# A delta-rule attention and mixture-of-experts layer, redesigned: attention state kept over x, paired inverses in small tiles, accumulating transfers, experts by batch, norms at the end

## The chip, the cores and the metric

One core of one Trainium2 chip. The time is that of one execution on the device in microseconds (us); of the kernel before, the median of three runs counts. Its engines are TensorE (PE: matmuls; PEld are its weight loads), VectorE (DVE), ScalarE (ACT), GpSimd (POOL) and SyncE (SP, which only issues transfers here).

## What is computed

```python
# B=2 sequences, S=2048 tokens, D=128; H=4 heads, DK=128, DV=32
q, k, v, beta = x @ Wq, x @ Wk, x @ Wv, sigmoid(x @ Wb)
k = k * rsqrt(sum(k*k, -1) + 1e-12);  q = q * DK**-0.5
# per head, over the tokens t of a sequence:
delta = (v_t - k_t^T S) * beta_t;  S = S + k_t delta^T;  o_t = q_t^T S
o = o * rsqrt(mean(o*o, -1) + 1e-5) * norm_w;  o = o * (g * sigmoid(g))   # g = x @ Wg
x1 = layernorm(x + o @ Wo)
# experts: E=8, F=448, top 2 of 8, capacity 640 for each batch and expert
probs = softmax(x1 @ gate_w.T);  slots = tokens of an expert in their order, first 640
y = (silu(slots @ w1) * (slots @ w3)) @ w2
out = layernorm(x1 + sum of y * probs over the token's two experts)
```

## The kernel before

The program is one block with a hand-written instruction stream for each engine, joined by semaphores.

**Attention (`phase_a`, 16 steps).** A step handles one chunk of 128 tokens of both sequences, so 8 pairs of sequence and head (`U = 8`). Within a chunk the recurrence is solved as a triangular system: A holds k times k below the diagonal, its inverse TT is built from 16x16 blocks on POOL (`solve`, 15 rounds of two operations, after a trip of the diagonal blocks through HBM), then joined on PE to 32, 64 and 128 wide (`z_32`, `w_32`, `z_64`, `w_64`, `z_128`, `w_128`, with a copy on DVE or ACT after each). The state St is kept as keys times deltas, 128x32 for each of the eight, and four groups of eight matmuls run over it and K (`ks`, `qs`, `t_r`, `k_d`, with `p_d` for the outputs inside the chunk). `step` writes PE's order by hand: what fills PSUM for chunk p+1 (`kt`, `k_tok`, `vb`, `kk`, `gate_t`, `qt`, `kq`) alternates with the inverse of chunk p and with the output of chunk p-1. An iteration of PE's loop holds two steps. All of this is float32, which the trace shows as two PE records for each matmul.

**Routing.** The output part of a step projects with Wo, adds x, normalises, turns x1 over (`x1_t`), forms the logits, takes the top two (`route`), counts tokens by expert with a triangular matmul (`cum`), and computes slots and gates (`place`). POOL scatters each token's row (four indirect transfers a step, `scatter`) into the table `slots_in`.

**Experts (16 units: eight experts for batch 0, then eight for batch 1).** A unit loads 640 slots and the expert's weights, turns the rows over (`flip`), forms both hidden matrices in 4 pieces of 112 features and 2 halves of 320 slots, each with three float32r matmuls (high and low halves of the split numbers: 48 matmuls of 320 columns), ACT takes Silu, DVE multiplies, and `down` multiplies with w2 (20 float32 matmuls, 40 records). PE has two PSUM banks for each of the two matrices. POOL writes the rows of the result back to the table `results` (five indirect transfers a unit, `send_back`).

**End.** `combine` reads x1 and the two expert rows of each token, adds them with the gates, and normalises; the combine of batch 0 runs beside the experts of batch 1, that of batch 1 after them, with a power on POOL (`c_rstd`) in each of 8 groups.

## Time and profile before

| what | us |
|---|---|
| median of 3 runs | 921.78 |
| range of the runs | 912.18 to 927.48 |
| span of the profiled execution | 911.5 |
| busy in it: PE / DVE / ACT / POOL | 752.7 / 419.9 / 337.6 / 398.9 |

The rows further down come from that one profiled execution. A row of the windows view gives for a stretch its length, each engine's busy time with its number of instructions, the clock that TensorE was granted as a share of 2.4 GHz, the share of the transfer engines and GB/s. A row of the timeline gives start, duration, engine, line, operation, output and inputs, shape, number of instructions merged, and in brackets the idle time before with what ended it. A row of the chain gives start, duration and what the chain that ended last was in.

### The profile page before, as it was taken

Reading aid. Unit: us, or ns where it says so; the run is one execution under the profiler, and the core shown is the slowest. Engines: PE = TensorE matmul, PEld = TensorE weight load, DVE = VectorE, ACT = ScalarE, POOL = GpSimd, SP = SyncE. Lnnn points to the kernel's source line nnn. Section 1 sums busy time; section 2 is a strip of 40 time slices with the busy share of each in tenths; the row PEclk is TensorE's granted clock in tenths of the full one; section 3 lists DMA queues with packets and bytes.
Section 4 is the critical chain, followed back from the end, with each engine's and each line's share of the span. In section 5 each row is a group of like instructions: output and inputs, shape, how many; then the busy total and the mean of one; then the engine's idle time right before and its main releaser. Section 6 shows DMA issues by size and latency. Waiting matters only on the chain.

```text
span 911.5 us, 19015 instructions
## 1 busy us (share of the span) xinstructions
PE 752.7 (83%) x6000; PEld 653.8 (72%) x6000; DVE 419.9 (46%) x1604; ACT 337.6 (37%) x1042; POOL 398.9 (44%) x794
## 2 busy tenths in 40 slices
PE   5398988988988989989989889753999999999700
PEld 4387877877877878778778778743888888887600
DVE  3135365455455453464462653413444546566444
ACT  3235345335335334254252451212343433434200
POOL 4444565474474562654653645121242433435321
PEclk9769799779779777788785795556999999999955
DMA  7342102111111111202201111012132324524042
GB/s 281 86 136 38 36 17 50 36 35 29 35 32 31 35 34 21 43 14 40 43 14 35 23 31 35 7 54 86 60 119 79 99 89 140 156 92 144 30 121 81
DMA packets 122469, 58.46 MB, mean 64 GB/s; under 512 B 73153, under 2 KB 115521, under 8 KB 122433
## 3 DMA queue, kind: packets, MB, share of 16 engines
q1 hardware_dynamic: 117824, 48.54, 20.7%
q0 software_dynamic: 4608, 9.48, 3.1%
q8 instruction: 18, 0.29, 0.1%
q14 instruction: 19, 0.15, 0.1%
HBM read 30.65 MB, written 27.34 MB: 64 GB/s over the span
## 4 chain that ended last, share of the span: by engine, by line
PE 55%; DVE 18%; issue 11%; ACT 8%; POOL 3%; DMA 3%; SPq 1%; DVEq 1%; ACTq 0%; POOLq 0%
PE ps L772 8%; PE ps L782 8%; PE ps L626 6%; PE ps L513 5%; PE ps L643 4%; PE ps L651 4%; DVE A L1167 3%; DVE hb L1243 3%; PE ps L523 3%; PE ps L615 3%; ACT hs L973 3%; PE ps L561 3%; PE ps L588 2%; ACT junk L827 2%; PE ps L635 2%
## 5 line engine op out<-in xcount | busy, mean ns | idle before, releaser
L1462 POOL DMA_INDIRECT results<-ye,row x80 | 81.4, 1018 | 160.3 <-ACT ye L979 124.9
L1243 DVE TENSOR_TENSOR hb<-ps,hs 112x320 f32<-112x320 f32 x128 | 62.8, 491 | 95.4 <-ACT hs L973 92.1
L772 PE MATMUL ps<-xeTh,w13h 128*112 128x320 f32 x256 | 88.1, 344 | 9.9 <-DVE hb L1243 7.4
L1397 POOL TENSOR_TENSOR prod<-ab,xs 64x15 f32<-64x15 f32 (+7 forms) x240 | 63.8, 266 | 69.3 <-DMA ab<-a_diag 51.8
L1428 POOL DMA_INDIRECT slots_in<-x,slot x64 | 63.2, 988 | 53.4 <-DVE gates L1232 37.5
L782 PE MATMUL ps<-w2s,hb 112*128 112x128 f32 x640 | 75.5, 277 | 9.8 <-DVE hb L1243 9.8
L782 PEld LDWEIGHTS ps<-w2s,hb 112*128 112x128 f32 x640 | 72.7, 192 | 13.4 <-DVE hb L1243 8.0
L772 PE MATMUL ps<-xeTl,w13h 128*112 128x320 f32 x256 | 79.7, 311 | 0.0
L772 PE MATMUL ps<-xeTh,w13l 128*112 128x320 f32 x256 | 79.6, 311 | 0.0
L973 ACT ACTIVATE hs<-ps 112x320 f32<-112x320 f32 x128 | 56.1, 438 | 62.6 <-PE ps L772 52.5
L1398 POOL TENSOR_TENSOR xs<-xs,prod 64x15 f32<-64x15 f32 (+7 forms) x240 | 66.8, 278 | 18.8
L1191 DVE TENSOR_TENSOR St<-St,ps 128x256 f32<-128x256 f32 x16 | 6.7, 421 | 127.7 <-PE ps L651 127.7
L772 PEld LDWEIGHTS ps<-xeTh,w13h 128*112 128x112 f32 x256 | 45.1, 176 | 27.7 <-DVE hb L1243 21.9
L513 PE MATMUL ps<-xTs,wk 128*128 128x256 f32 x128 | 50.5, 563 | 8.2 <-DMA xTs<-xT 8.2
L1404 POOL TENSOR_TENSOR osq<-o 128x256 f32<-128x256 f32 x16 | 9.8, 612 | 103.6 <-ACT o L861 103.6
L626 PE MATMUL ps<-St,KT 128*128 128x32 f32 x256 | 54.3, 385 | 0.0
L867 ACT ACTIVATE KT<-ps 128x512 f32<-128x512 f32 x32 | 19.1, 597 | 93.6 <-PE ps L513 93.6
L626 PEld LDWEIGHTS ps<-St,KT 128*128 128x128 f32 x256 | 52.6, 313 | 0.1
L561 PE MATMUL ps<-QT,KT 128*128 128x128 f32 x256 | 46.6, 340 | 6.2 <-ACT QT L851 6.2
L513 PEld LDWEIGHTS ps<-xTs,wk 128*128 128x128 f32 x128 | 35.8, 294 | 20.2 <-issue 13.2
L1417 POOL TENSOR_TENSOR m<-A,mask 128x1024 f32<-128x1024 f32 x16 | 37.6, 2348 | 23.0 <-DVE A L1167 23.0
L561 PEld LDWEIGHTS ps<-QT,KT 128*128 128x128 f32 x256 | 39.9, 238 | 8.2 <-ACT QT L851 8.1
(188 smaller groups left out, 1657.1 us busy)
## 6 DMA issues: line engine op xcount, KB each, us to landing
w<-w SPq DMA_DIRECT2D x32, 224.0 KB, 3.3
slots_in<-zeros SPq DMA_DIRECT2D x10, 516.0 KB, 5.4
xe<-slots_in SPq DMA_DIRECT2D x16, 322.5 KB, 3.3
results<-zeros SPq DMA_DIRECT2D x8, 512.0 KB, 5.9
yc<-results SPq DMA_DIRECT2D x32, 128.0 KB, 2.6
w2s<-w SPq DMA_DIRECT2D x16, 224.0 KB, 3.0
xTs<-xT SPq DMA_DIRECT2D x16, 128.0 KB, 3.4
a_diag<-A SPq DMA_DIRECT2D x64, 32.0 KB, 1.6
```

Of the source, the lines that this page charges most:

```text
L513: last = mm(ps[:, fill_bank[g], 256 * k:256 * k + 256], wk[:, DK * h:DK * h + DK], xTs[:, par, :], start=True, stop=True)
L561: last = mm(ps[:, fill_bank[10 + j], P * h:P * h + P], KT[:, par, h, P * j:P * j + P], QT[:, par, h, P * j:P * j + P], start=True, stop=True)
L626: last = mm(ps[:, CB, DV * u:DV * u + DV], KT[:, par, h, P * j:P * j + P], St[:, u, :], start=True, stop=True)
L772: last = mm(ps[0:FW, 2 + 2 * k + g, 0:HALF], wp[:, par, k, FW * c:FW * c + FW], xp[:, par, cols], start=(t == 0), stop=(t == 2))
L782: last = mm(ps[:, 6 + i // 4, P * (i % 4):P * (i % 4) + P], hb[:, par, c, P * i:P * i + P], w2s[:, par, c, :], start=(c == 0), stop=(c == ...
L973: af(hs[:, s % 2, :], ps[0:FW, 2 + s % 2, 0:HALF], ACT.Silu).then_inc(hs_ready, 1)
L1243: v.tensor_tensor(hb[:, par, c, HALF * g:HALF * g + HALF], ps[0:FW, 4 + g, 0:HALF], hs[:, g, :], ALU.mult).then_inc(h_ready, 1)
L1397: link(g.tensor_tensor(pr_, bc(ab[:, j + 1:, j], 2, j + 1), bc(xs[:, 0, j, 0:j + 1], 1, n), ALU.mult))
L1398: link(g.tensor_tensor(xs[:, 0, j + 1:, 0:j + 1], xs[:, 0, j + 1:, 0:j + 1], pr_, ALU.subtract))
L1417: g.tensor_tensor(m32[:], A[:, par], bc(mask32[:], 1, U), ALU.mult).then_inc(m32_ready, 1)
L1428: g.indirect_dma_start(out=xs_d[:, :], out_offset=bass.IndirectOffsetOnAxis(ap=at, axis=0), in_=x1[:, par, j, k, :], in_offset=None).then_ ...
L1462: g.indirect_dma_start(out=y_d[b][:, :], in_=ye[:, par, i, :], in_offset=None, out_offset=bass.IndirectOffsetOnAxis(ap=row[:, par, i:i + 1 ...
```

## The change

The kernel is rewritten; names below are of the changed kernel.

- **State.** `Mk = Wk Wk^T` and `Nq = Wq Wk^T` are formed once for each head. `y = Mk x` and `gq = Nq x` take the place of keys and queries, so key-times-key is x times y, and the state Zs is x times delta: one 128x128 matrix for each sequence, for all heads, updated by two matmuls that accumulate in PSUM (`new_state`). Key norms come from the diagonal of A, read back from HBM with one more transfer. The projections by Mk, Nq, Wg and Wb are three float32r matmuls each from chunk 5 on.
- **Inverses.** Each 16x16 solve covers two chunks on 128 partitions (`solve`, POOL; the first chunk's on DVE). `z_32`, `w_32`, `z_64`, `w_64` work on 32x32 tiles, `z_128` and `w_128` on 64x64 tiles that lie on the diagonal of the array. The masked copies of A on POOL and of the 16x16 blocks on DVE are gone.
- **Order.** The attention loop is written out for all engines, 25 passes, in which up to seven chunks are in work; PE's idle stretches at two places get matmuls that write nothing used (`keep_on`: 22 in pass 4, 9 and 36 in pass 21).
- **Projection.** x is added by a matmul (`project_x`), and the logits come out of the same matmul as the projection, so `x1_t` and `logits` go.
- **Transfers.** Slots are scattered by transfers that add to a zeroed table, apart from the last chunk's, and carry the gate; expert rows, scaled by the gate on ACT, are added by transfers straight to `x1_store`. The table `results` and its zeroing go.
- **Experts.** An expert serves batch 0 and then batch 1 with one load of its weights. The 448 features are three pieces of 128 and one of 64; the two 64-wide pieces share a matmul: 42 instead of 48. Five PSUM banks go round for the hidden pieces.
- **End.** Only a layernorm over 8 groups of 4 tiles of 128 rows is left, with its square root on ACT; batch 0's rows wait only for batch 0's transfers.

The diff, cut to its core:

```diff
-            def k_d(p, par):
-                pe.wait_ge(d_ready, p + 1)
-                for u in range(U):
-                    j, h = u // H, u % H
-                    last = mm(ps[:, CB, DV * u:DV * u + DV], K[:, par, j, DK * h:DK * h + DK], dl[:, u, :],
-                              start=True, stop=True)
-                last.then_inc(chain_mm, 1)
+            def products(to, whole, parts, n):
+                if n < XF:
+                    return mm(to, whole, xTs[:, :, cols(n)], start=True, stop=True)
+                hi, lo = parts
+                r = n % XR
+                mm(to, hi, xhs[:, r], start=True, stop=False)
+                mm(to, hi, xls[:, r], start=False, stop=False)
+                return mm(to, lo, xhs[:, r], start=False, stop=True)
...
+            def z_32(n):
+                pe.wait_ge(xh_out, n + 1)
+                wait(pe, t128_out, n)
+                apart(pe)
+                for u in range(U):
+                    for k in range(4):
+                        s = slice(32 * k, 32 * k + 32)
+                        last = mm(ps[s, LV, 16 * u:16 * u + 16], A[s, n % AR, u, s], xh[s, n % 2, u, :],
+                                  start=True, stop=True)
...
+            def new_state(p):
+                for b in range(B):
+                    last = mm(ps[:, ZA, P * b:P * b + P], xk[:, b, p, :],
+                              dl[:, H * b:H * b + H, :].rearrange("p h d -> p (h d)"),
+                              start=(p == 0 and b == 0), stop=True, skip_group_check=True)
...
+            for p in range(NP + LAST):
+                at(values, p - 1)
+                at(turn_keys, p - 5)
+                at(z_128, p - 5)
+                at(key_key, p - 1, 0)
+                at(project, p - 6)
+                at(key_query, p - 5, 1)
+                at(w_128, p - 5)
+                at(gate_in, p - 4)
+                at(queries, p - 4, 0)
+                at(deltas, p - 5)
+                at(state_queries, p - 5)
+                at(queries, p - 4, 1)
+                at(turn_deltas, p - 5)
+                at(key_key, p - 1, 1)
+                at(count, p - 6)
+                at(z_32, p - 4)
+                at(outputs, p - 5)
+                at(project_x, p - 5)
+                at(keys, p, 0)
+                at(w_32, p - 4)
+                at(new_state, p - 5)
+                at(key_query, p - 4, 0)
+                at(z_64, p - 4)
+                at(head_sums, p - 5)
+                at(state_keys, p - 4)
+                at(keys, p, 1)
+                at(w_64, p - 4)
...
-                    g.indirect_dma_start(out=y_d[b][:, :], in_=ye[:, par, i, :], in_offset=None,
-                                         out_offset=bass.IndirectOffsetOnAxis(ap=row[:, par, i:i + 1], axis=0)
-                                         ).then_inc(y_back[par], 16)
+                    pool.wait_ge(ye_ready, CT * n + i + 1)
+                    apart(pool)
+                    g.indirect_dma_start(out=x1_d[:, :], in_=ye[:, par, i, :], in_offset=None,
+                                         out_offset=bass.IndirectOffsetOnAxis(ap=row[:, par, i:i + 1], axis=0),
+                                         compute_op=ALU.add).then_inc(y_back[par], 16)
...
+            for g in range(NT // LG):
+                if g % (NP // LG) == 0:
+                    sp.wait_ge(y_back[g // (NP // LG)], 16 * CT * E)
+                sp.dma_start(rows_l[:, tiles_of(g), :], rows_[:, tiles_of(g), :]).then_inc(rows_ld[g], 16)
```

PE, around the state update of a steady attention step, before (L643 `t_r`, L523 `k_tok`, L651 `k_d`, L660 `p_d`, L530 `vb`, L539 `kk`):

```order
L643 MATMUL ps<-R,TT 128x32 x8
L58 REGISTER_ALU
L523 MATMUL ps<-wk,xTs 128x512
L651 MATMUL ps<-dl,K 128x32 x8
L660 MATMUL ps<-PT,dl 32x128 x8
L58 REGISTER_ALU
L523 MATMUL ps<-wk,xTs 128x512
L58 REGISTER_ALU
L530 MATMUL ps<-wvb,xTs 128x132 x2
L58 REGISTER_ALU
L539 MATMUL ps<-KT 128x128 x4
```

The same place now, in pass 18 (L859 and L863 `count`, L708 `z_32`, L831 `outputs`, L846 `project_x`, L718 `w_32`, L820 `new_state`, L694 `key_query`, L728 `z_64`, L837 `head_sums`, L776 `state_keys`, L738 `w_64`):

```order
L859 MATMUL ps<-M,rest 128x16
L863 MATMUL ps<-M,tri 128x16
L708 MATMUL ps<-xh,hb 32x16 x32
L831 MATMUL ps<-PT,dl 32x128 x8
L846 MATMUL ps<-rx,xTs 128x136 x2
L718 MATMUL ps<-z,xi 32x16 x32
L820 MATMUL ps<-dl,xk 128x128 x2
L694 MATMUL ps<-gq,xTs 128x512
L728 MATMUL ps<-x32T,hb 32x32 x16
L837 MATMUL ps<-osq,heads 128x256
L776 MATMUL ps<-y,Zs 32x128 x8
L738 MATMUL ps<-z,x 32x32 x16
```

The eight matmuls of the state update (L651) have become two (L820), and the steps of the inverse, which were eight matmuls over all 128 rows, are 32 or 16 of 32x32 tiles, each separated from the next by full-width work.

POOL in the expert loop of batch 1, before (L1462 writes expert rows, L1468 is the power of the last norm):

```order
L1462 DMA results<-ye,row 5376x128 x5
L1467 REGISTER_ALU
L1468 TENSOR_TENSOR rstd_c<-ve,minus_half 128x2
L1457 REGISTER_ALU
L58 ISA
```

and now, where L1706 adds to `x1_store` and each row waits for its own copy on ACT (L1704):

```order
L1706 DMA x_store<-xk,row 5376x128
L1704 REGISTER_ALU
L1706 DMA x_store<-xk,row 5376x128
L1704 REGISTER_ALU
L1706 DMA x_store<-xk,row 5376x128
```

The five transfers are no longer issued as one piece, and nothing of the norm stands between two units.

## Rows read from the trace of the kernel before

**Rows 1.** The windows view, four stages: attention, hand-over, experts, end

```profile
42.00:588.00 546.00, 502.32 (x4335) 432.86 (x4335) 252.81 (x1047) 222.79 (x747) 277.05 (x626) 0.80 0.18 38
588.00:630.00 42.00, 18.53 (x105) 15.36 (x103) 10.58 (x55) 6.52 (x21) 10.02 (x11) 0.50 0.24 75
630.00:862.00 232.00, 213.69 (x1483) 192.34 (x1483) 123.66 (x355) 93.41 (x220) 81.61 (x82) 0.99 0.32 99
862.00:912.00 50.00, 0.00 (x0) 0.00 (x0) 21.84 (x90) 0.72 (x2) 11.12 (x14) 0.54 0.32 93
```

**Rows 2.** The timeline of PE, one attention step (128*32 is the weight tile)

```profile
436.14 1.11 PE L606 MATMUL ps<-TT,A 64*64 64x64 f32 x16 [0.74 <-DVE x L1097]
...
442.80 3.60 PE L626 MATMUL ps<-St,KT 128*128 128x32 f32 x16
...
451.75 1.10 PE L523 MATMUL ps<-wk,xTs 128*128 128x512 f32 x2
452.69 1.87 PE L651 MATMUL ps<-dl,K 128*128 128x32 f32 x16
454.49 0.64 PE L660 MATMUL ps<-PT,dl 128*32 128x128 f32 x16
...
464.89 1.12 PE L588 MATMUL ps<-xh,A 64*64 64x32 f32 x32 [0.88 <-ACT xh L886]
...
467.44 0.69 PE L597 MATMUL ps<-z,x 64*32 64x32 f32 x32
```

**Rows 3.** The windows view of PE in that step: busy time, granted clock

```profile
439.00:440.00 1.00, 1.00 (x6) 0.50 0.00 0
...
468.00:469.00 1.00, 0.61 (x14) 1.00 0.35 32
```

**Rows 4.** The groups of ACT by line: count, busy us, mean ns

```profile
L891 ACT ACTIVATE TT<-x32T 32x256 f32<-32x256 f32 x64 | 26.5, 414 | 0.9
L825 ACT ACTIVATE K<-ps 128x512 f32<-128x512 f32 x32 | 19.2, 599 | 40.2 <-PE ps L651 36.7 <-PE ps L523 3.5
```

**Rows 5.** The groups of DVE by line

```profile
L1177 DVE TENSOR_TENSOR PT<-ps,upper 128x512 f32<-128x512 f32 x32 | 22.2, 692 | 6.0 <-PE ps L561 5.3
...
L1104 DVE TENSOR_TENSOR r<-ps,xk 128x256 f32<-128x256 f32 x16 | 6.8, 425 | 7.6 <-PE ps L674 7.1
```

**Rows 6.** The groups of POOL by line

```profile
L1462 POOL DMA_INDIRECT results<-ye,row x80 | 81.4, 1018 | 160.3 <-ACT ye L979 124.9 <-issue 27.3 <-DVE row L1255 8.2
L1398 POOL TENSOR_TENSOR xs<-xs,prod 64x15 f32<-64x15 f32 (+7 forms) x240 | 66.8, 278 | 18.8
```

**Rows 7.** The chain, from the 16x16 blocks to the first joining matmul

```profile
36.58 2.46 DMA inv<-xs
39.05 3.20 DMA xi<-inv
42.39 3.57 PE ps L570 x16
```

**Rows 8.** The chain, from the last count to the first expert matmul

```profile
614.64 0.07 PE ps L695 x2
...
621.82 2.42 DMA slots_in<-x,slot
```

**Rows 9.** The chain in one expert unit

```profile
843.08 4.73 PE ps L782 x40
847.81 0.90 PE ps L772 x6
848.73 0.45 ACT hs L973
849.20 0.50 DVE hb L1243
```

**Rows 10.** The chain, the last down product and after

```profile
857.18 4.75 PE ps L782 x40
...
868.81 0.97 POOL results L1462
```

2014 lines of the change are left out of this document (1076 added, 938 removed).

## The prediction

> **What bounds the kernel now.** I read the windows view first, to cut the span into stages, then PE's timeline inside an attention step, then the chain of waits where the stages meet. The windows [rows 1] show 546 us for 16 attention steps (34.1 us each), of which PE is busy 502, DVE 253, POOL 277, ACT 223; then 42 us in which the last chunk is finished, scattered and loaded again; 232 us for 16 expert units (14.5 each), PE busy 214; and 50 us at the end with PE idle. The first 42 us are the way to the first inverse: the 16x16 solve goes out, comes back, and PE's first joining matmul starts at 42.39 [rows 7]. So both long stages are PE's. In the step the reader is to see what a record costs back to back at the full clock: two records of 512 columns take 0.94 us (0.47 each, from 451.75 to 452.69), sixteen with 128x128 weights and only 32 columns 1.80 (0.1125 each, 452.69 to 454.49), sixteen with 32-wide weights and 128 columns 0.58 (0.64 less the overlap of 0.06) [rows 2]. Narrow outputs over full weights pay for the weights. The same work at the half clock takes double: L626 took 3.60 us [rows 2], beside a granted clock of 0.50 at 439 us, where PE was fully busy, and 1.00 at 468, where it was busy 0.61 [rows 3]. Over the stage the clock averages 0.80 [rows 1]. Priced like this, the records of a step add up to about 27 us, so 34.1 is that times 1.26: some 3 us of idle time (PE busy 92%) and 4 or more for the clock.
>
> **The attention step after.** Full-width work: 24 float32r matmuls of 256 columns for keys and queries and 6 for gate and beta. The float32r matmul of 320 columns costs 0.15 (six in 0.90 [rows 9]), so 256 columns cost 0.12: 3.6 us. Products of x with y and gq are four float32 matmuls of 512 columns, 8 records at 0.47: 3.8. Values and new state, 8 records of 128 columns at 0.1125: 0.9; both projections, 8 of 136 columns at 0.12: 1.0; head sums, two of 256 columns at half of 0.47: 0.5; four transposes and the count: 0.7. Together 10.5. Four groups of eight with 32-wide weights and 128 columns at 0.58 [rows 2]: 2.3. The inverse: 192 records on 32x32 tiles, of 16 and of 32 columns. The nearest row is L597, 32-wide weights, 32 records in 0.69, 0.020 each after the overlap of starts; L588 with 64-wide weights has 0.036 [rows 2]. That is 3.9 to 6.9; I take 3.9, as the tile is that of L597. The two 64x64 stages, 32 records, cost between 0.036 (L588) and 0.069 (L606, 16 in 1.11): 1.1 to 2.2, I take 1.6. Sum 18.3 us, between 17.8 and 21.9.
>
> The other engines must fit below it. ACT: six copies of 512 columns at 0.60, some 20 operations of 256 columns at 0.41 [rows 4] and ten small ones at 0.2 to 0.3: 14.3. DVE: two at 0.69, some 17 of 128 to 256 columns at up to 0.425 [rows 5], and 30 small ones of 0.1 to 0.2: about 15. POOL: 30 solve operations at 0.278 and a gap of 0.08 (18.8 us over 240), halved since one solve serves two chunks: 5.4; values and Silu 1.4, scatter four times 1.36 (1.018, and 27.3 us of issue over 80 [rows 6]): 12.5 in all. The masks of A and of the blocks go and free these engines, worth nothing by itself while PE is the bound.
>
> Nothing hides PE's own waits. Each stage of the inverse hands over to DVE or ACT and back; in the new order 1 to 2.5 us of other matmuls stand between each two, and a copy costs 0.4 to 0.9, so most fits. Before, the step was its records times 1.26 with clock and waits, and times 1.09 with the idle share alone. These give 23.1 and 19.9; between them I take 21.5.
>
> A rule and a row can be weighed here. The rows above give 0.020 us for a record of the 32-wide tiles [rows 2]. The Trainium skill (TensorE: Matmul & The Clock Gate, "Wait — 56ns, not 53.3ns?") states that start-to-start never drops below about 25 ns however small the matmul. By it the 192 records of the inverse would cost 4.8 us instead of 3.9 and the kernel 14 us more. The measurement decides, and my sum keeps 0.020.
>
> **The sum.** (1) To the first joining matmul: before, 42.39, of which the solve on POOL ended at 36.58 and store and load took 2.46 and 3.20 [rows 7]. Now keys are a product of x alone and the first solve is on DVE, where its 30 operations take some 0.2 to 0.25 each against 0.36: about 36. The rest of that pass, without outputs and in a chain with DVE, is 7: 43. (2) Passes 5 to 15 are full: 11 x 21.5 = 237. (3) Pass 16 lacks the keys, 20; passes 17 to 19 lack keys, values and key-key too (1.4 + 0.8 + 1.9 less): 3 x 17.4 = 52. (4) The last chunk from the end of its inverse to its count is a chain of some 15 hand-overs: 13. That is 365. (5) Count to first hidden matmul: before, from 614.7 past the scatter's landing (621.82 + 2.42 [rows 8]) to the start of the experts at 630 [rows 1] 15.6; now two of the four transfers and three of five tiles must be in: 12. (6) A unit: 42 matmuls at 0.15 = 6.2, the flip's five transposes 0.7, down 4.73 [rows 9]: 11.6. The old stalls, 14.5 less 12.6 of work, come from six matmuls waiting behind Silu 0.45 and product 0.50 [rows 9] with two banks for each matrix; five banks in a ring leave 2.2 us of matmuls before the first reuse, so I leave 0.2: 11.8, times 16 = 189. ACT and DVE have some 6.5 us in it, five transfers at 1.36 on POOL 6.8. Fewer weight loads gain nothing more. (7) End: the transfers of the last unit are out 5.5 us after PE (before, the last was issued at 868.81, 6.9 after the down product's end at 861.93 [rows 10]), land 2.4 later, batch 1's first rows are loaded 3 later, four groups at 2.0 on DVE (128-column statistics at 0.3 by [rows 5]), and the last scaling and store 4.5: 24 instead of 50. Batch 0's groups lie beside the last unit. Total 43 + 237 + 20 + 52 + 13 + 12 + 189 + 24 = 590 against the profiled span of 911.5. The median of the runs shown, 921.8, is 1.011 times that, so 596.
>
> Costed at nothing: the key norms' extra transfer, the adding of x and the loads of all x, covered by a chunk's lead of several passes (if that lead were short the inverse would come late, below); the matmuls that write nothing used, in stretches that wait anyway. The price of an accumulating transfer is in no row: from below the plain one's 1.36 us, and no gain; from above I have only the space POOL leaves. I take the plain price, the nearest row. At twice it a unit would need 13.6 on POOL: 29 us more, and 7 at the end.
>
> **The rivals.** *The clock falls in each step (0.15).* Before, it stood at half for some 10 us of a step after a stretch of gaps and tiny matmuls [rows 2, 3]. If the small tiles bring the same, 10 us at half clock do 5 us of work: +5 on 15 steps, 590 + 75, by the median 672. Against it: the gaps before were waits for DVE (0.74 and 0.88 us [rows 2]), which I expect shorter.
>
> *Hand-overs bind (0.15).* The engines' own orders interlock, or each of the ten tile groups costs 0.3 to 0.4 us as PE goes over between tile shapes: 25 us a step, +56, 652. For it: ACT and DVE are busy 14 and 15 of 21.5. Against: L660's sixteen records between full-width groups took 0.58 in all [rows 2]. The Trainium skill (TensorEngine Tiling (Array Packing), Key Properties) says that changing the tiling mode drains TensorE; the row shows that whatever that costs lies inside the 0.58, some 0.15 above sixteen records of 0.027.
>
> *It fits better (0.12).* A step of 19 and a unit of 11.6 with nothing lost: -37 and -3, 555.
>
> *Accumulating transfers bind: slower than before (0.02).* With x us each, POOL needs 4x + 7 in a step and 5x in a unit. Above 3.6 the step and above 2.4 the unit follow it. The excess is 16(4x + 7 - 21.5) + 16(5x - 11.8) = 144x - 421, which eats the gain of 322 at x = 5.2, 3.8 times the plain one.
>
> **How the numbers follow.** The forecast, 596, has 0.56, with its own range of 565 to 635: a step between 19.9 and 23.1 (-25 to +24), a doubled transfer's +36, and five to ten us for the start. The range from 550 to 668 adds the better case and the hand-overs, and leaves most of the clock's case and what lies below out. A measurement of this kernel tells about 2% from no change. Faster by more: 0.97; within 2% 0.01, some mixture of the rivals; slower 0.02, the transfers.
>
> **What would show it.** In the changed profile: passes of 21 to 22 us with PE busy over 90% and a clock above 0.95 (the clock's rival: near 0.8); `z_32` and `w_32` at 0.6 to 0.7 us per 32 records (double: tile changes); the first `z_32` near 36 us; units of 11.8 us whose hidden matmuls wait for nobody; accumulating transfers near 1.02 us on POOL; 24 us after the last down product. The prediction is wrong if a PE wait on ACT or DVE of over a microsecond stands in every pass, if PE waits for the load of the inverse, or if POOL is busy throughout a unit.

## The result

| what | us |
|---|---|
| changed kernel, median of 4 runs | 540.24 (539.42 to 542.46) |
| kernel before, median of the 4 runs beside it | 921.47 (912.18 to 927.48) |
| ratio | 0.588, 95% interval 0.5845 to 0.5915 |
| profiled span of the changed kernel | 537.7, mean granted clock 0.961 |
| busy in it: PE / DVE / ACT / POOL | 490.4 / 330.7 / 332.4 / 319.7 |

The kernel is faster, as forecast, but by more: 540 lies 56 us below the forecast of 596 and 10 below the range. Here is the windows view of the changed kernel, its columns as in [rows 1] (length; busy time and instructions of PE, PEld, DVE, ACT, POOL; granted clock; share of the transfer engines; GB/s). It is cut near the first joining matmul, at the last full passes, the last count, the first hidden matmul and the end of the experts:

```profile
0.00:37.00 37.00, 31.46 (x145) 23.04 (x146) 16.55 (x82) 19.03 (x41) 9.74 (x36) 1.00 0.38 64
37.00:271.00 234.00, 229.53 (x4735) 167.24 (x4733) 168.94 (x719) 171.07 (x489) 154.77 (x304) 1.00 0.53 87
271.00:319.00 48.00, 40.07 (x757) 29.62 (x757) 33.04 (x154) 25.52 (x78) 24.95 (x18) 0.82 0.45 71
319.00:331.30 12.30, 9.22 (x78) 8.63 (x78) 2.97 (x14) 2.04 (x7) 6.29 (x6) 1.00 0.43 83
331.30:513.00 181.70, 180.09 (x1387) 179.84 (x1387) 97.49 (x271) 99.35 (x254) 118.04 (x77) 0.99 0.47 79
```

In the attention of before the clock averaged 0.80 and a step was 34.1 us [rows 1]; now the clock is 1.00 and PE is busy for 98% of the second row. The first count of a pass comes at 194.56 us and the next at 211.78: a steady pass is 17.22 us. The timeline of PE in the changed kernel over that pass (start, duration, engine, line, operation, operands, weight tile, shape, records), of which the small-tile groups and two others are shown, answers to [rows 2]:

```profile
194.66 0.73 PE L708 MATMUL ps<-xh,hb 32*32 32x16 f32 x64
195.32 0.64 PE L831 MATMUL ps<-PT,dl 128*32 128x128 f32 x16
...
199.42 0.69 PE L728 MATMUL ps<-x32T,hb 32*32 32x32 f32 x32
200.04 0.70 PE L837 MATMUL ps<-osq,heads 128*128 128x256 f32 x2
...
203.99 0.68 PE L750 MATMUL ps<-TT,hb 64*64 64x64 f32 x16
204.60 1.12 PE L679 MATMUL ps<-y,xTs 128*128 128x512 f32 x2
...
211.88 0.72 PE L708 MATMUL ps<-xh,hb 32*32 32x16 f32 x64
```

From the start of a group to the start of the next: 64 records on 32x32 tiles with 16 columns take 0.66 us, 0.0103 each; 32 of them with 32 columns 0.62, 0.0195 each; sixteen on 64x64 tiles 0.61. No row of the pass has a bracket with a wait in it. The expert units show the same: the chain of the changed kernel lies on PE alone (start, duration, what the chain was in), where that of before went over ACT and DVE [rows 9]:

```profile
344.88 5.57 PE ps L956 x38
350.45 0.55 PE ps L914 x5
351.00 4.47 PE ps L970 x40
355.46 6.17 PE ps L956 x42
```

A unit is 11.17 us: hidden 6.16, the turned rows 0.55, down 4.47. Last, the chain from the last down product to the end, which answers to [rows 10]; the 3.06 us of POOL's queue in it are no other work, since POOL's transfers of 512.71 and 514.56 run in that time:

```profile
506.96 4.48 PE ps L970 x40
...
513.04 3.06 POOLq L184
...
516.40 1.54 POOL x_store L1706
...
518.25 3.30 DMA x_store<-xk,row
521.57 2.84 DMA xTs<-x_store
```

Adding transfers take POOL longer than the plain ones of [rows 6], 1.55 us against 1.018. The page of the changed kernel lists them by line (busy us, mean ns, idle before and what ended it); with some 0.30 between two of them POOL's part of a unit is 5 x 1.85 = 9.2 of 11.17 us, so it is not in the way:

```profile
L1706 POOL DMA_INDIRECT x_store<-xk,row x80 | 123.9, 1549 | 68.5 <-ACT xk L1214 45.8
```

### The profile page after: what moved, and what is told of

The parts are those of the page before. It is cut to its first block, busy times and chain, and to the rows that moved or that the text cites. A ratio compares the mean times of both kernels' runs of the same rounds, so it can differ in the third digit from the quotient of the medians.

```text
span 537.7 us, 18954 instructions
## 1 busy us (share of the span) xinstructions
PE 490.4 (91%) x7096; PEld 408.4 (76%) x7096; DVE 330.7 (61%) x1316; ACT 332.4 (62%) x916; POOL 319.7 (59%) x441
## 4 chain that ended last, share of the span: by engine, by line
PE 71%; DMA 9%; POOL 7%; issue 5%; SPq 3%; ACT 2%; DVE 1%; POOLq 1%; ACTq 0%; DVEq 0%
PE ps L956 19%; PE ps L970 13%; PE ps L694 4%; PE ps L679 4%; POOL slots_in L1665 3%; PE ps L650 3%; PE ps L653 3%; PE ps L654 2%; PE ps L655 2%; POOL xs L1648 2%; PE ps L914 2%; PE ps L718 2%; POOL prod L1647 2%; DMA a_diag<-hb 1%; PE ps L728 1%
## 5 line engine op out<-in xcount | busy, mean ns | idle before, releaser
L1706 POOL DMA_INDIRECT x_store<-xk,row x80 | 123.9, 1549 | 68.5 <-ACT xk L1214 45.8
L1540 DVE TENSOR_TENSOR hb<-ps,hs 128x320 f32<-128x320 f32 (+1 forms) x128 | 62.7, 491 | 53.1 <-ACT hs L1206 52.6
L1206 ACT ACTIVATE hs<-ps 128x320 f32<-128x320 f32 (+1 forms) x128 | 55.7, 435 | 34.5 <-PE ps L956 33.5
L970 PE MATMUL ps<-w2s,hb 128*128 128x128 f32 x640 | 74.1, 275 | 0.0
L970 PEld LDWEIGHTS ps<-w2s,hb 128*128 128x128 f32 x640 | 72.8, 192 | 0.0
L956 PE MATMUL ps<-xeTh,w13h 128*128 128x320 f32 x224 | 71.3, 318 | 0.9 <-DVE xeTl L1564 0.9
L956 PE MATMUL ps<-xeTl,w13h 128*128 128x320 f32 x224 | 69.9, 312 | 0.0
L956 PE MATMUL ps<-xeTh,w13l 128*128 128x320 f32 x224 | 69.9, 312 | 0.0
L956 PEld LDWEIGHTS ps<-xeTh,w13h 128*128 128x128 f32 x224 | 42.8, 191 | 1.1 <-issue 1.1
L956 PEld LDWEIGHTS ps<-xeTl,w13h 128*128 128x128 f32 x224 | 42.8, 191 | 0.0
L694 PE MATMUL ps<-gq,xTs 128*128 128x512 f32 x64 | 34.5, 623 | 0.3 <-issue 0.3
```

What stands on the lines that cost most here:

```text
L694: mm(ps[:, to, :], xTs[:, b, cols(n)], gq[:, n % 2, b].rearrange("p h t -> p (h t)"), start=True, stop=True).then_inc(fill_mm, 1)
L956: last = mm(ps[:, HB[fill % 5], 0:HALF], w_[:, P * c:P * c + P], x_[:, par, cols], start=(t == 0), stop=(t == 2))
L970: last = mm(result_at(i), hb[:, par, c, P * i:P * i + P], w2s[:, we, c, :], start=(c == 0), stop=(c == FC))
L1206: af(hs[to, s % 4, :], ps[src, HB[fill_of(s) % 5], 0:HALF], ACT.Silu).then_inc(hs_ready, 1)
L1540: v.tensor_tensor(hb[rows_, par, c, HALF * g:HALF * g + HALF], ps[rows_, at, 0:HALF], hs[rows_, s % 4, :], ALU.mult).then_inc(h_ready, 1)
L1706: g.indirect_dma_start(out=x1_d[:, :], in_=ye[:, par, i, :], in_offset=None, out_offset=bass.IndirectOffsetOnAxis(ap=row[:, par, i:i + 1], ...
```

## The experiments

Runs of one heading were made on one chip, beside runs of the kernel before. The unedited changed kernel was run beside the first comparison and once more as the control of the fourth series; in the other series a difference from it goes from one chip to another, and differences of a few us between them are not safe. In all diffs the names are those of the changed kernel.

### Series 1: what a pass is made of (kernel before: 921.24)

**Tiles in turn.** In `z_32` and `w_32` all eight matmuls of one diagonal tile (16 of the 64 records) go before those of the next tile, instead of one matmul for each of the four tiles in rotation.

```diff
-                for u in range(U):
-                    for k in range(4):
+                for k in range(4):
+                    for u in range(U):
```

> The changed kernel with the two 32x32 joining stages issued tile by tile (the eight matmuls of one diagonal tile, then the next tile) in place of round the four tiles; same matmuls, same result. In the changed kernel 64 such records take 0.66 us, 0.0103 each. Theory 1 (four tiles work at the same time, and that is why the term was half of what I priced from a row with two tiles): the records of one tile queue behind each other, so 64 records take at least twice as long, 1.3 us or more; a pass of 17.2 us grows by 1.3 us or more, the kernel by 16 to 45 us. Rival (the records are cheap because their weights are 32 columns and the output 16, wherever they lie): 0.66 us as before, no change.

Measured: 581.49 (575.7 to 583.68), ratio 0.6279 (0.6214 to 0.6345), 41 us more. The timeline of PE in this kernel:

```profile
174.72 1.89 PE L708 MATMUL ps<-xh,hb 32*32 32x16 f32 x64
176.54 0.64 PE L831 MATMUL ps<-PT,dl 128*32 128x128 f32 x16
```

The same 64 records take 1.82 us, 0.0284 each instead of 0.0103. Two groups of them and 1.17 more in each make 2.34, and the pass is 19.56 instead of 17.22, with PE busy throughout. So records on different tiles of the diagonal run side by side; whether it is the matmuls or their weight loads that overlap is not separated. Over 16 passes the 2.34 us are 37, which is also the difference of the ratios; by medians it is 41.

**More matmuls.** `z_32` does its 64 records twice.

```diff
+                for u in range(U):
+                    for k in range(4):
+                        s = slice(32 * k, 32 * k + 32)
+                        last = mm(ps[s, LV, 16 * u:16 * u + 16], A[s, n % AR, u, s], xh[s, n % 2, u, :],
+                                  start=True, stop=True)
                 last.then_inc(z32_mm, 1)
```

> The changed kernel with the first 32x32 joining stage issued twice in each pass (64 more PE records of 0.0103 us, the same values written again). Theory 1 (the steady pass is nothing but PE's stream, every wait is covered): each of 16 passes grows by 0.66 us, the kernel by 8 to 11 us, to about 550. Rival (the hand-overs to the copying engines set the pass, and PE only looks busy): under 3 us.

Measured: 560.06 (555.16 to 569.25), ratio 0.6038 (0.5982 to 0.6095), 20 us more by medians and 15 by ratios. The best passes are 17.7 to 17.9, what the records cost. Others are longer, by gaps that no semaphore ends, some of them inside groups of small records, as in this timeline of PE:

```profile
116.42 0.48 PE L713 MATMUL ps<-xh,hb 32*32 32x16 f32 x34 [1.44 <-issue]
...
194.64 0.44 PE L723 MATMUL ps<-z,xi 32*32 32x16 f32 x32 [0.90 <-issue]
```

The 64 records account for 16 x 0.66 = 10.6 us. The profile is that of the slowest of the four runs (569.25), so it shows what kind of gap there is but not how much of the rest such gaps are in the other runs. Their cause is open.

**More on ACT.** One more copy of 512 columns for each half of a chunk's A, into a tile that nobody reads.

```diff
+                link(af(more[:], ps[:, src, :], ACT.Copy))
                 af(A[:, n % AR, H * b:H * b + H, :], ps[:, src, :].rearrange("p (h t) -> p h t", h=H),
```

> The changed kernel with one more copy of 512 columns on ScalarE ahead of each of the two key-key copies of a pass, into a spare tile: 1.3 us more in each of 16 passes on an engine busy 12.6 of 17.2. Theory 1 (waits of PE are covered with room to spare): under 4 us on the kernel. Rival, the factor of my forecast (a pass is its records times 1.1 to 1.26, because the copies come late): each late copy is seen by PE, 10 to 20 us.

Measured: 542.9 (541.63 to 545.75), ratio 0.5866 (0.5818 to 0.5913). ACT has 1.2 us more in a pass (two copies of 0.597) and the pass is 17.46, 0.24 more. ACT is covered.

**Much more on DVE.** Three such copies ahead of each mask of `kq`, so that DVE has about 16.5 of 17.2 us.

```diff
+                link(v.tensor_copy(more[:], ps[:, bank("kq", n, b), :]))
+                link(v.tensor_copy(more[:], ps[:, bank("kq", n, b), :]))
+                link(v.tensor_copy(more[:], ps[:, bank("kq", n, b), :]))
```

> The changed kernel with three more copies of 512 columns on VectorE ahead of each of the two masked products of a pass, into a spare tile: about 4 us more in each pass on an engine busy 12.4 of 17.2, so 16.5 of 17.2 if nothing waited. Theory 1 in its plain form (busy time decides while it is below PE's): under 5 us on the kernel. Rival (order decides: a copy that is 2 us late stalls PE although VectorE has time left): PE waits in each pass, 1 to 4 us of them, and if such gaps bring the half clock as in the kernel before, more: 20 to 100 us, with a granted clock below 0.9 over the passes.

Measured: 572.21 (568.76 to 573.39), ratio 0.6178 (0.6123 to 0.6232). Passes are 18.6 and 19.5 us in turn. The waits of PE in this kernel (us in total, times, longest):

```profile
PE ps L740 <- DVE z L1327: 21.2, 16, 2.0
PE ps L655 <- DVE PT L1396: 5.1, 8, 1.1
```

With DVE nearly full, what hands back an inverse stage comes late in most passes, 1.3 us in the mean of 16 waits. The clock stayed at 1.00 from 60 to 240 us all the same: these waits did not bring the half clock. The attention of the unedited kernel has DVE at 12.4 of 17.2 us and PE waits for it in no steady pass; that slack is what keeps the hand-overs hidden.

### Series 2: the half clock after the last full pass (kernel before: 921.16)

In the third row of the windows above the clock averages 0.82. Of the changed kernel, unedited, cut finer, and the waits around the fall in the timeline of PE:

```profile
277.00:283.00 6.00, 3.92 (x109) 2.93 (x98) 2.74 (x11) 2.51 (x9) 4.26 (x5) 0.53 1.10 252
283.00:289.00 6.00, 6.00 (x64) 3.37 (x66) 2.77 (x7) 2.74 (x7) 4.48 (x3) 0.50 0.58 65
```

```profile
276.49 0.91 PE L708 MATMUL ps<-xh,hb 32*32 32x16 f32 x64 [1.41 <-DVE xh L1302]
282.31 0.52 PE L718 MATMUL ps<-z,xi 32*32 32x16 f32 x24 [2.03 <-issue]
```

PE waits 1.41 us there (DVE for the load of the inverses), in pass 18, right after the count at 274.9. The clock stands at half from 278 to 294; the gap of 2.03 us comes after it has fallen. At the same time SP sends the first two experts' weights.

**Weights later.**

```diff
-                if p == NP + 1:
+                if p == NP + 3:
                     load_weights(0, 0)
                     load_weights(1, 1)
```

> The changed kernel with the first two experts' weight loads issued in pass 19 in place of pass 17. In the changed kernel these 1.3 MB go out at 274.3 to 277.8 us, ahead of the next load of an inverse on SyncE, while PE has a gap of 2.03 us in the middle of a group of 64 records that no semaphore explains, and the clock is at half from 277.6 to 294. Theory 2 (the burst of transfers holds up PE's instructions and one inverse, and this costs some 2 us in gaps and, if it is what brings the clock down, 8 us more): 3 to 10 us faster, no gap inside a group. Rival (the fall of the clock comes from the wait of 1.41 us for the inverse at 276.5, before the burst): half clock stays, under 3 us faster. Second rival: the weights now come late for the experts or collide with the last scatters: slower by 1 to 5 us.

Measured: 536.03 (532.97 to 540.26), ratio 0.581 (0.5778 to 0.5843). The half clock is still there:

```profile
283.00:289.00 6.00, 5.66 (x86) 3.25 (x84) 3.18 (x8) 2.59 (x8) 4.62 (x3) 0.50 0.45 38
```

The burst of weights does not bring it.

**Seven idle products.** They were meant for the place where PE waits 1.41 us. The expectation has that wait in pass 17; it is in pass 18, so the products stand one pass ahead of it.

```diff
+                if p == NP + 1:
+                    pe.wait_ge(t128_out, NP - 3)
+                    for _ in range(7):
+                        mm(ps[:, LV, 3 * P:4 * P], ident[:], ident[:], start=True, stop=True)
                 at(z_32, p - 4)
```

> The changed kernel with seven matmuls of 128 columns that write an unused region, ahead of the first 32x32 stage in pass 17, where PE waits 1.41 us for an inverse (14 records, 1.6 us at the full clock). Theory 2 in its second form (the idle gap brings the half clock from 277.6 to 294 us, in which 8 us of work take 16): clock stays at 1.00, 5 to 8 us faster. Rival (the gap of 2.03 us and the transfers' burst do it): half clock comes all the same some us later, no gain or 1 us slower.

Measured: 532.06 (529.59 to 543.12), ratio 0.5758 (0.5726 to 0.5789). The products in PE's timeline, and two windows of this kernel:

```profile
261.88 1.81 PE L901 MATMUL ps<-ident 128*128 128x128 f32 x14
```

```profile
270.00:277.00 7.00, 6.04 (x61) 4.08 (x54) 6.22 (x32) 2.42 (x9) 6.23 (x6) 0.76 0.73 91
283.00:289.00 6.00, 5.18 (x108) 3.36 (x107) 4.89 (x17) 3.86 (x11) 4.93 (x5) 1.00 0.50 63
```

The products end at 263.7, a pass ahead. PE comes later to pass 18 and finds its inverse there: the group that had waited starts at 279.28 without a wait. The clock falls all the same, but earlier and for 3 us (272.3 to 275.5) instead of 16, and the last count is at 314.6 instead of 319.0. So this run does not show that the idle stretch brought the half clock, nor that filling it would take it away: nothing filled it. What made the fall short is open, and the run without any idle products, below, had a short one too.

**Both.** The weights later and the seven products together.

> Both edits of the two runs before: weights in pass 19 and the seven matmuls in pass 17. Theory 2: 8 to 11 us faster than the changed kernel, 529 to 532, clock 1.00 from 60 to 315 us. Rival (only the wait for the inverse counts): as the run with the seven matmuls alone.

Measured: 531.39 (529.84 to 534.99), ratio 0.5757 (0.5729 to 0.5785), as with the idle products alone. The clock is at half from 272.3 to 275.5 here too.

**No idle products at all.** The kernel's own 67 (22 in pass 4, 9 and 36 in pass 21) go.

```diff
-                for _ in range(n):
+                for _ in range(0):
```

> The changed kernel without the 67 matmuls that write nothing used (22 in pass 4, 9 and 36 in pass 21). They lie in stretches in which PE waits anyway. Theory 1: they hold the clock, so without them pass 4 and the first passes, and then the first expert unit, run partly at the half clock: 3 to 8 us slower. Rival: they do nothing, under 1.5 us.

Measured: 538.41 (536.37 to 542.35), ratio 0.585 (0.5808 to 0.5891). The clock does fall without them, to 0.54 from 37 to 43 us and 0.50 from 316 to 332, where it was 1.00; the median is within 2 us of the unedited kernel's. But the half clock of pass 18 lasted 6 us here instead of 16 (278 to 284, after a wait of 2.33 us), and the last count came at 314.9, 4 us earlier, so the median does not price the products. By stages: the first joining matmul starts at 36.72 instead of 37.32, where the 22 products had kept PE busy until then; the first count comes at 72.9 instead of 71.9 us (72.0 to 73.2 in the other kernels of this series), from the last count to the first hidden matmul it is 12.6 instead of 12.4 us, and the units take 180.9 instead of 180.1 (181.1 with "Weights later", which has the products and starts its units at half clock all the same). In those stretches PE waits for others, and its clock is worth 2 us at most.

### Series 3: width, ring, way back, end (kernel before: 910.87)

**All products in float32.** The projections of chunks 5 and on are no longer split into three float32r products.

```diff
-                if n < XF:
+                if n < NP:
                     return mm(to, whole, xTs[:, :, cols(n)], start=True, stop=True)
```

> The changed kernel with the projections by Mk, Nq, Wg and Wb left as float32 matmuls for all chunks (two records each in place of three of float32r); the splitting on ScalarE and VectorE stays. A float32r matmul of 256 columns costs 0.12 us in the trace, three of them 0.36; float32 ones 0.26 or less each record by the passes before chunk 5 (four records in 1.06). Theory 1 (PE's stream sets the pass): ten products a pass cost 0.15 to 0.17 more each, +1.6 us on some 11 passes, 13 to 20 us slower. Rival (columns count alone, a float32 record of 256 at 0.213): +0.07 each, 6 to 9 us slower. If the hand-overs set the pass: no change.

Measured: 556.45 (551.08 to 559.27), ratio 0.6089 (0.603 to 0.6148). Passes average 18.8 us. A record of 512 columns costs 0.47 [rows 2], so an estimate for a float32 product of 256, two records, is the same 0.47, where three float32r ones cost 0.36; with ten of them in a pass that is 1.1. The neighbours in this series, which leave this part alone, average 17.9, so it measures 0.9: the size of PE's work. The expectation's 1.6 came from 0.26 a record; four records take 0.95 in this trace.

**A ring of three banks** for the hidden pieces instead of five.

```diff
-                        old, m = (fill - 5, n) if fill >= 5 else (10 + fill if fill < 4 else 9, n - 1)
+                        old, m = (fill - 3, n) if fill >= 5 else (10 + fill if fill < 4 else 9, n - 1)
```

> The changed kernel with PE waiting, before each hidden piece, for the piece three before it to be read in place of five before it, so as if three PSUM banks went round. Theory 3 (the old unit's 2 us of stalls came from too few banks between PE and the Silu and product behind it, and five banks removed them): PE stalls come back, 0.3 to 0.5 us at several of the 14 pieces, 2 to 4 us a unit, 30 to 60 us slower. Rival (the stalls went because VectorE no longer does the combine and ScalarE less of the weights): under 5 us.

Measured: 568.94 (568.22 to 573.0), ratio 0.626 (0.6214 to 0.6306). The chain of this kernel in a unit goes back over ACT and DVE, as that of before did:

```profile
374.22 1.33 PE ps L956 x9
...
375.58 0.45 ACT hs L1206
...
376.05 0.50 DVE hb L1540
```

A unit is 12.8 us instead of 11.17: 1.6 x 16 = 26 us. By medians it is 24 us above the control of series 4. The ring of five is what let the units stand at their own work.

**Plain transfers on the way back.** The sum of the residual and the second expert is left out.

```diff
-                                         compute_op=ALU.add).then_inc(y_back[par], 16)
+                                         compute_op=ALU.bypass).then_inc(y_back[par], 16)
```

> The changed kernel with the expert rows written over x1_store by plain indirect transfers in place of added, so the sum of x1 and of the second expert is left out. It measures what adding costs. In the changed kernel an adding transfer takes POOL 1.54 us and lands in 3.3, against 1.02 and 2.7 of the plain ones in the kernel before. Theory 4 (POOL has room in a unit, 9.2 of 11.2 us, so only the last transfers are on the path): 1.5 to 4 us faster, all of it at the end. Rival (the adding transfers also slow the units by their load on the queues): units shorter than 11.17 us, 5 to 10 us faster.

Measured: 567.01 (562.14 to 577.59), ratio 0.6199 (0.6138 to 0.6261). Both theories fell: a transfer takes POOL 0.97 us instead of 1.55, and the kernel is slower, 22 us above the control of series 4. Units are 11.2 to 15.6 us instead of 11.17, with gaps of up to 1.7 us in which PE, ACT and DVE stand still together (seven over 0.3 us from 376 to 450; none in the unedited kernel from 376 to 420). Series 4 and 5 are about that.

**End apart.** No group of rows is loaded before the transfers of both batches are in.

```diff
-                if g % (NP // LG) == 0:
-                    sp.wait_ge(y_back[g // (NP // LG)], 16 * CT * E)
+                if g == 0:
+                    sp.wait_ge(y_back[0], 16 * CT * E)
+                    sp.wait_ge(y_back[1], 16 * CT * E)
```

> The changed kernel with the first rows of the last norm loaded only when all expert rows are in, as for the second half, so batch 0's four groups no longer lie beside the last unit. In the changed kernel the last four groups take 1.87 us each, set by the scaling on ScalarE. Theory 5 (the end is one pipeline of 1.87 us a group): 4 x 1.87, 7 to 8 us slower. Rival (the end is set by the transfers' latencies, the groups lie in them): under 3 us.

Measured: 550.85 (549.89 to 554.7), ratio 0.6058 (0.6012 to 0.6103). From the last down product to the end it is 33.3 us instead of 26.3, four groups of 1.87 on ACT: their hiding beside the last unit is worth 7 us.

### Series 4: control, repeats and the plain scatter (kernel before: 914.71)

**Control.** The changed kernel as it is.

> The changed kernel itself, nothing edited, beside the other kernels of this call. In the last group of runs the passes of attention took 17.6 and 18.2 us in turn where the first run had 17.22 throughout, in three kernels that left those passes as they are, with some five gaps of 0.7 to 0.9 us ahead of a group of small records that no semaphore explains. Theory A (the gaps belong to the chip or the hour): they may be here again with nothing edited, and all kernels of a call carry the same 5 to 8 us. Theory B (they belong to the program, to where its instructions lie): 540 us and 17.22 us a pass here, whatever the other kernels show.

Measured: 544.71 (541.22 to 551.38), ratio 0.5952 (0.5894 to 0.601). With nothing edited, every other pass now has a gap that no semaphore ends; timeline of PE:

```profile
119.56 0.68 PE L750 MATMUL ps<-TT,hb 64*64 64x64 f32 x16 [0.80 <-issue]
```

There are five of 0.6 to 0.9 us before that line between 60 and 260 us, and PE is busy 97.13 of the 100 us from 100 to 200, against 100.00 in the first profile. Theory A holds for these gaps: the same program has them with one chip or hour and not with another. They can come with an edit too: "More matmuls" had such gaps on the chip on which "More on ACT" had none over 0.4 us between 100 and 240 us. The control is 4.5 us above the first median, and the same gaps stand in the profiles of series 3, so about that much of its differences is theirs.

**Plain way back, again.**

> The rows brought back by plain writes instead of adding ones, a second time (the sum of the residual and of the second expert is left out). Theory A (the 27 us of the first time belong to that chip or hour): within 3 us of the control of this call, or a little below. Theory B (the plain write itself makes it slower, by gaps in which PE, ACT and DVE all wait for no semaphore): again 20 to 30 us above the control, with gaps of 1 to 2.5 us in the hidden products of the units and about 12 to 13 us a unit instead of 11.17.

Measured: 570.87 (564.27 to 572.95), ratio 0.6226 (0.617 to 0.6282), 26 us above the control. The plain form itself is slower: Theory B.

**Both edits of series 2, again.**

> Seven idle products in the last pass of attention, and the burst of expert weights two passes later, a second time, beside the control. Both theories: 6 to 9 us below the control by medians (531.4 against 540.2 before), at a clock of 1.00 from 277 to 294 us.

Measured: 544.65 (542.31 to 549.57), ratio 0.5966 (0.5911 to 0.6021), level with the control; both theories expected a gain. The half clock in the control was already shorter (285 to 291.5 us), and with the edits it came at two other places, 0.58 from 260 to 264 and 0.56 from 294 to 300. A gap of 1.79 us before 278.7 did not bring it (1.00 from 276 to 280), where one of 0.96 us at 270.6 came ahead of the fall in "Seven idle products". So what brings it after the last full pass stays open, the low medians of series 2 are not shown to be the edits' doing, and no version here is shown to beat the changed kernel.

**Plain scatter.**

```diff
-                                             compute_op=ALU.bypass if last else ALU.add
+                                             compute_op=ALU.bypass
```

> All rows go to their slots by plain writes instead of adding ones; the attention part is as it was otherwise. This leaves out the sum by which a slot keeps both of its writers. Theory A (a transfer's kind sets only POOL's time, and POOL is covered): 540 us as the control, POOL 1.0 us a transfer instead of 1.55, passes 17.22. Theory B (plain indirect writes bring gaps in the supply of instructions, as in the units of the plain way back): passes longer by gaps without a releaser, 5 to 20 us in all over the control.

The expectation calls a sum left out; none is. A slot that is read has one writer, so writing it and adding onto zeros give the same row.

Measured: 616.53 (615.59 to 617.73), ratio 0.6754 (0.6709 to 0.6799): 72 us above the control, for transfers that are each 0.57 us shorter on POOL. The timelines of POOL, DVE and ACT in one pass of this kernel (in brackets the idle time before; "remote" is a wait whose end the trace does not explain):

```profile
124.27 0.99 POOL L1665 DMA_INDIRECT slots_in<-x,slot  x1 [0.15 <-issue]
125.57 0.97 POOL L1665 DMA_INDIRECT slots_in<-x,slot  x1 [0.30 <-issue]
126.85 0.98 POOL L1665 DMA_INDIRECT slots_in<-x,slot  x1 [0.30 <-issue]
128.13 0.97 POOL L1665 DMA_INDIRECT slots_in<-x,slot  x1 [0.30 <-issue]
```

```profile
130.22 0.85 DVE L1325 COPY z<-ps 32x256 f32<-32x256 f32 x2 [4.62 <-remote]
...
130.27 0.47 ACT L1098 ACTIVATE oln<-ps,eps 128x256 f32<-128x256 f32 x1 [4.18 <-remote]
```

The matmuls that DVE and ACT wait for had ended at 125.49 and 126.12. Both engines stand still until 130.2, 1.1 us after POOL's last transfer, and PE's own records stutter (gaps of 0.3 and 0.44 at 127 and 128.3) before it waits for DVE for 2.4 us. From 60 to 271 us there are eight such stops of 1.2 to 4.2 us that overlap a run of transfers; the unedited kernel has no time over 1.2 us in which DVE and ACT are both idle. The clock then falls too: after a stop it is at half for some 7 us (0.50 from 181 to 186 and from 205 to 210), 0.86 on average from 100 to 200. A pass is 23.9 instead of 17.2; an estimate from the mean of 0.86 is that a good 3 us of these 6.7 are the clock's, the rest the stops.

### Series 5: the pace or the kind (kernel before: 913.06)

**Plain scatter, paced.** A copy on POOL between one transfer and the next.

```diff
+                        if j or k:
+                            link(g.tensor_copy(pace[:].rearrange("p (u c) -> p u c", u=2), bc(ident[:], 1, 2)))
-                                             compute_op=ALU.bypass if last else ALU.add
+                                             compute_op=ALU.bypass
```

> The plain scatter once more, with a POOL copy of 128x256 (0.61 us) between one transfer and the next, so that the four of a pass start 1.9 us apart as the adding ones do, instead of 1.28. The sum over a slot's writers is left out as in the plain scatter, whose passes took about 23 us with DVE and ACT both still from 1.4 to 1.8 us after the first plain transfer's start until the last one's end. Theory C (the pace of the plain transfers does it): the stops vanish, passes of 17.2 to 17.8, 540 to 550 us. Theory D (the kind of transfer does it at any pace): DVE and ACT stop again in each pass, 600 us or more.

Measured: 538.21 (536.11 to 541.97), ratio 0.5919 (0.5863 to 0.5976). A little more work on POOL took 78 us off the plain scatter (0.6754 to 0.5919 by ratios): no stop is left, and a pass is 17.2 again. The copy took 0.41 in the median and not 0.61, so the transfers start 1.7 to 1.8 us apart instead of 1.28, as the timeline of POOL in this kernel shows:

```profile
136.34 0.99 POOL L1669 DMA_INDIRECT slots_in<-x,slot  x1 [0.28 <-POOL pace L1668]
137.32 0.53 POOL L1668 COPY pace<-ident 128x256 f32<-128x256 f32 x1
138.13 1.00 POOL L1669 DMA_INDIRECT slots_in<-x,slot  x1 [0.28 <-POOL pace L1668]
```

**Half plain.**

```diff
-                                             compute_op=ALU.bypass if last else ALU.add
+                                             compute_op=ALU.bypass if last or j else ALU.add
```

> Of the four transfers of a pass the first two add and the last two are plain, at the program's own pace (part of the sum over a slot's writers is left out). Theory C (a row of plain transfers in quick succession): two in a row end about 2.3 us after the first's start, so the stop has hardly begun: under 10 us in all over the control, 545 to 555. Theory D (each plain transfer has its price): half of the 72 us of the plain scatter, 575 to 585.

Measured: 538.37 (536.2 to 539.23), ratio 0.5924 (0.5871 to 0.5977). Two plain transfers in a row, 1.29 us apart, bring no stop. POOL's timeline in this kernel has both kinds side by side:

```profile
134.41 1.63 POOL L1665 DMA_INDIRECT slots_in<-x,slot  x1 [0.16 <-issue]
136.34 1.59 POOL L1665 DMA_INDIRECT slots_in<-x,slot  x1 [0.30 <-issue]
138.24 0.99 POOL L1665 DMA_INDIRECT slots_in<-x,slot  x1 [0.30 <-issue]
139.53 0.99 POOL L1665 DMA_INDIRECT slots_in<-x,slot  x1 [0.30 <-issue]
```

Theory C holds and D falls: it is a run of four or five plain transfers at 1.28 us that stops the engines in this kernel, not a plain transfer as such (three in a row were not tried). What stops them is open. The trace names no releaser, loads of instructions do not line up with the stops, and the pace alone is not enough either: in the kernel before, four plain transfers stood 1.28 us apart too, and the matmuls beside them went at their usual pace, 1.87 us for the group of [rows 2]. DVE and ACT were waiting for those matmuls then, so a stop of these two would not be seen there (timelines of POOL and PE of the kernel before):

```profile
136.97 0.97 POOL L1428 DMA_INDIRECT slots_in<-x,slot  x1 [0.30 <-issue]
138.25 0.96 POOL L1428 DMA_INDIRECT slots_in<-x,slot  x1 [0.30 <-issue]
```

```profile
137.90 1.87 PE L651 MATMUL ps<-dl,K 128*128 128x32 f32 x16
```

The paced version was not tried on the way back.

## Why the prediction was wrong where it was

The mechanism was right: both long stages are PE's, ACT, DVE and POOL fit below it, and the gain comes from fewer and cheaper records, from the clock and from the end. A factor on the length of a pass was wrong. By the terms of the sum:

| term | forecast | measured |
|---|---|---|
| (1) first joining matmul; end of that pass | 36; 43 | 37.3; 45.0 |
| (2) passes 5 to 15 | 237 | 192.3 |
| (3) passes 16 to 19 | 72 | 68.0 |
| (4) last chunk to its count | 13 | 13.8 |
| (5) count to first hidden matmul | 12 | 12.4 |
| (6) 16 units | 189 | 180.1 |
| (7) end | 24 | 26.3 |
| span | 590 | 537.7 |

**The failed step is "between them I take 21.5" in (2).** The records had been summed to 18.3 us and then multiplied by 1.09 to 1.26, the share that clock and waits had in the step of before [rows 1]. A steady pass has neither: PE is busy all of 17.22 us at clock 1.00. Of the 45 us that (2) was too high, 11 x 3.2 = 35 are this factor and 11 x 1.1 = 12 are the sum itself, less some longer first passes. (3) carried the same factor, which a stretch of half clock in pass 18 hides. The prediction gave the reason why the waits could go, 1 to 2.5 us of other matmuls between any two stages of the inverse, and then did not believe it: it carried over a ratio from a kernel whose order had no such filling. Series 1 shows how that order stands: ACT's extra 1.2 us cost 0.24, and only DVE at 16.5 of 17.2 us brought waits of a microsecond back. The rival "it fits better" (a step of 19, 555 us, chance 0.12) was the nearest case and still too high, since it too kept a factor above the sum; so the range ended at 550.

**The 32-wide records were mis-sized inside the sum.** The forecast took 0.020 for all 192, from L597, "as the tile is that of L597"; but that row has 64x32 tiles and 32 columns [rows 2], not 32x32. The two groups of 64 cost 0.0103 each record, the two of 32 0.0195: 2.6 us instead of 3.9. The two 64x64 stages cost 1.2 instead of 1.6, near the lower bound. All other records come to 13.4 instead of 12.8. The rule of the Trainium skill quoted there (TensorE: Matmul & The Clock Gate, "Wait — 56ns, not 53.3ns?"), a floor of about 25 ns between starts, would have taken the sum further off: the pass shows 10 ns. With the tiles in turn the trace shows 28 ns. The Trainium skill has both halves (TensorE: Matmul & The Clock Gate): beside that floor, its "Part 3: Packing small matmuls" says that matmuls on different tiles of the array overlap, some 4 ns from one start to the next. The overlap is what the first trace and the tiles in turn show for four diagonal tiles; the 4 ns are not: from start to start it is 10.3 ns in the mean. The 25 ns hold for the records that go tile by tile (28.4) and not, as the page puts it, for every matmul. The forecast should have read the second place beside the first.

**The clock.** Its rival did not come in the full passes. It came once, in pass 18, for some 16 us at half clock. In the two profiles in which the fall lasted 3 and 6 us the last count came 4.4 and 4.1 us earlier.

**Changes of tile shape**, the reason given for the rival of binding hand-overs, cost nothing that can be told from the records: six small-tile groups stand between full-width ones in each pass, and 64 of the smallest records take 0.66 us with whatever the change costs. No row shows the 0.027 us that the prediction sets beside L660; the same kind of group takes 0.57 from start to start here (195.32 to 195.89).

**The units.** 11.17 against 11.8. The 0.2 left for stalls was not needed: the ring of five bridges them, and that of three brings 1.6 a unit. Hidden matmuls are 0.147 each and the turned rows 0.55 instead of 0.7; down was 4.47 instead of 4.73.

**Accumulating transfers** were taken at the plain price. They cost 1.85 us with their issue instead of 1.36, which is 1.36 times as much and between the bounds, and land in 3.3 us instead of 2.4. POOL stays below PE, so only the end pays: the last transfer starts 6.8 us after the down product (511.44 to 518.25), where the forecast had 5.5, and lands 3.3 later. That is 2.2 of the 2.3 us between 24 and 26.3. That plain ones would be slower by up to 72 us here was no part of any rival.

**Start and hand-over** (36, 7, 13, 12) were right within 1.5 us each: chains priced hand-over by hand-over came out well; what was priced by a ratio did not. Of the 1.3 us on the first joining matmul 0.6 are the idle products ahead of it.

**The last step**, from span to median, took 1.011 from before; the profiled run's own is 1.003 and the median's 1.005, 3 us of the difference.

## What to carry to other kernels

Sum a stage that one engine bounds from its own records, and add a wait only where a named hand-over finds less other work ahead of it than it takes; the stall share of the old order says nothing of the new one. Send small matmuls to the tiles of the array in rotation, not tile by tile. Where an engine's transfers are covered, look at what else runs while they are issued before making them cheaper, and check in the trace that an edit stands at the wait it is meant for, since a better time alone does not show it. Measure such a fix on more than one chip, with the unedited kernel beside it.

## What the runs showed of the hardware that was not expected

- Four 32x32 tiles on the diagonal, in rotation: 0.0103 us from record to record with 16 columns; the same records tile by tile: 0.0284.
- An indirect transfer that adds holds POOL 1.55 us instead of 0.97 to 1.02, and lands in 3.3 us (expert rows; the plain ones of the kernel before in 2.7).
- Four or five plain indirect transfers 1.28 us apart came with stops of DVE and ACT and gaps in PE. In the pass shown, DVE and ACT went on 1.1 us after the end of the last one. The kernels were 72 and 26 us slower, the half clock after the stops included. 1.7 us apart, or two at a time, plain scatters brought no stop. The cause is open.
- The same program had no gaps in its passes on one chip and gaps of 0.6 to 0.9 us in every other pass on another, 540.2 against 544.7 us by medians, and these gaps have no releaser in the trace.
